# Small loads ahead of x, the first scale table shared between GpSimd and VectorE, later tables cut into pieces, and one more hidden tile prepared ahead, in a two-FFN-and-attention kernel on Trainium2

## What is computed

```
x = x + 0.5 * FFN(layernorm(x))
x = x + Attention(layernorm(x))        # one head of 128, softmax over 1024 keys, with biases
x = x + 0.5 * FFN(layernorm(x))        # the same FFN weights

FFN(x) = (silu(x @ Wg) * (x @ Wu)) @ Wd          # 512 -> 1376 -> 512
W[k, n] = scales[g_idx[k], n] * (w4[k, n] - (z4[g_idx[k], n] + 1))
```

## Time and profile before

| | us |
|---|---|
| median of 3 runs | 855.09 |
| lowest, highest | 853.18, 855.42 |
| the profiled execution, its own time | 856.05 |
| its span in the trace | 854.2 |
| TensorE busy | 831.7 (97%) |
| VectorE busy | 484.9 (57%) |
| ScalarE busy | 273.0 (32%) |
| GpSimd busy | 247.9 (29%) |

### The profile page before, as it was taken

The page is one execution under the profiler, slowest core; times in us unless marked ns, Lnnn a source line. Parts: engine busy times, 40 slices in busy tenths (PEclk is TensorE's granted clock), DMA queues, the critical chain, the costliest instruction groups (busy, mean ns, idle before and its releaser), DMA issues.

```text
span 854.2 us, 10686 instructions
## 1 busy us (share of the span) xinstructions
PE 831.7 (97%) x4006; PEld 675.2 (79%) x4006; DVE 484.9 (57%) x807; ACT 273.0 (32%) x469; POOL 247.9 (29%) x205
## 2 busy tenths in 40 slices
PE   4899999999999999999999999999999999999998
PEld 3676768887888888788888888888888888888786
DVE  5878664654845454464967686545445744434452
ACT  3222332453421121241574783111212512112221
POOL 6634431552210533030234463150510201101100
PEclk9999999999999999999999999999999999999999
DMA  5767656985484534142115146845344064444121
GB/s 149 213 228 225 220 167 216 356 316 191 179 315 143 162 135 144 57 161 86 62 62 168 67 162 251 314 136 172 125 149 162 25 221 137 159 148 150 39 95 54
DMA packets 71177, 139.28 MB, mean 163 GB/s; under 512 B 24485, under 2 KB 35413, under 8 KB 66133
## 3 DMA queue, kind: packets, MB, share of 16 engines
q1 hardware_dynamic: 65858, 131.22, 45.9%
q10 hardware_dynamic: 5138, 6.95, 2.5%
q0 software_dynamic: 128, 0.41, 0.2%
HBM read 100.52 MB, written 37.95 MB: 162 GB/s over the span
## 4 chain that ended last, share of the span: by engine, by line
PE 71%; DVE 2%; DMA 1%; ACT 1%; issue 0%; POOL 0%; SPq 0%; ACTq 0%; POOLq 0%; DVEq 0%
PE ps L774 37%; PE ps L781 31%; PE ps L792 2%; PE ps L1184 1%; DMA xn<-stream 1%; DVE xn L1706 1%; DMA stream<-xres 0%; DVE stats L1683 0%; DVE pT L1672 0%; ACT pr L1532 0%; POOL t L2172 0%; ACT oT L1299 0%; DVE oT L1672 0%; DVE t L1672 0%; DVE hT L1672 0%
## 5 line engine op out<-in xcount | busy, mean ns | idle before, releaser
L774 PE MATMUL ps<-blk,ring 128*128 128x512 f32 (+1 forms) x1386 | 321.1, 390 | 0.1
L774 PEld LDWEIGHTS ps<-blk,ring 128*128 128x128 f32 (+1 forms) x1386 | 256.6, 185 | 58.4 <-DVE blk L1672 0.5
L781 PE MATMUL ps<-wd,hT 128*128 128x512 f32 (+1 forms) x1056 | 250.8, 392 | 0.9 <-DVE hT L1672 0.8
L781 PEld LDWEIGHTS ps<-wd,hT 128*128 128x128 f32 (+1 forms) x1056 | 196.8, 188 | 43.5 <-DVE hT L1672 1.2
L2215 POOL TENSOR_TENSOR h<-h,u 128x512 f32<-128x512 f32 (+1 forms) x33 | 42.8, 1297 | 325.7 <-ACT h L1425 325.7
L781 PE MATMUL ps<-xT,wp 128*128 128x512 f32 x480 | 117.2, 399 | 0.2 <-DVE xT L1672 0.2
L781 PEld LDWEIGHTS ps<-xT,wp 128*128 128x128 f32 x480 | 89.3, 190 | 21.9 <-issue 2.2
L1675 DVE TENSOR_TENSOR u<-ps,p1s 128x512 f32<-128x512 f32 (+1 forms) x66 | 45.4, 688 | 97.3 <-PE ps L774 97.3
L1425 ACT ACTIVATE h<-h 128x512 f32<-128x512 f32 (+1 forms) x33 | 20.9, 632 | 176.8 <-DVE h L1675 176.8
L1675 DVE TENSOR_TENSOR u<-ps,u 128x512 f32<-128x512 f32 (+1 forms) x66 | 45.6, 691 | 26.2 <-PE ps L774 25.2
L1675 DVE TENSOR_TENSOR h<-ps,p1s 128x512 f32<-128x512 f32 (+1 forms) x33 | 22.8, 691 | 63.7 <-PE ps L774 63.7
(11 more groups left out here) (132 smaller groups left out, 892.0 us busy)
## 6 DMA issues: line engine op xcount, KB each, us to landing
ring<-wsaved SPq DMA_DIRECT2D x29, 1024.0 KB, 5.1
ring<-wsaved SPq DMA_DIRECT2D x33, 768.0 KB, 4.4
wsaved<-wp SPq DMA_DIRECT2D x10, 1024.0 KB, 4.7
stream<-xres SPq DMA_DIRECT2D x32, 256.0 KB, 2.3
xn<-stream SPq DMA_DIRECT2D x8, 1024.0 KB, 7.5
xres<-stream SPq DMA_DIRECT2D x32, 256.0 KB, 3.7
wfull<-wf ACTq DMA_DIRECT2D x20, 256.0 KB, 2.5
wsaved<-wp SPq DMA_DIRECT2D x10, 512.0 KB, 3.1
```

The costliest lines, as they stand in the source:

```text
L774: mm = pe.matmul(ps[0:w, bank, :], ring[:, slot, which, a, kt, 0:w], blk[:, which, b, kt, :], start=not onto and kt == 0 and n == 0, stop= ...
L781: mm = pe.matmul(bank_ap, lhs(a), rhs(b), start=first and n == 0, stop=last and n == 2)
```

## The change

1. **Constants** move from GpSimd to VectorE, in front of everything VectorE did; there are eight increments of `s_cst` now.
2. **Loads.** On ScalarE's queue, `grp` and the gate scales (after `s_cst` 2) go ahead of x. SyncE loads only the up scales there. Unit 3 moves behind `table_d(0)`.
3. **Piece 0 of the scale table**: GpSimd makes `left`, VectorE makes `table` in one instruction. GpSimd cuts the down scales before its first power, not after its second.
4. **VectorE's order at the start**: the one-hot ahead of the statistics; `table` of piece 0 and `unpack(0)` ahead of the second `ln_shift`; piece 1 right behind `dequantise(0)`, ahead of `rows_lo`.
5. **Pieces 2 and 3** are split: `left` at tiles 2 and 4, `table` at tiles 3 and 5, each at the head of the tile.
6. **GpSimd's one-hot work for down** goes one unit earlier: the first columns before `w_lo(1)`, clamp of the rest before `w_lo(2)`, compare before `w_lo(3)`.
7. **keep_warm** 8 instead of 6 at the start.
8. **Bottom of pair 0**: block 1's fourth hidden tile is split in `plain_bottom`; ScalarE does its part between the two copies of the last weight block. Slots and the wait for them change with it.

```diff
-            return e % 3 if e < NT + 2 else (0, 2, 1)[e % 3]
+            return e % 3 if e < NT + 2 else (1, 2, 0)[e % 3]
-            return e - 1 if e == NT + 2 else e - 2
+            return e - 1 if e in (NT + 2, NT + 3) else e - 2
-        FIRST_STEPS, CUT_STEPS, ZERO_STEPS, SCALE_STEPS = 4, 5, PACK + 1, 2
+        FIRST_STEPS, CUT_STEPS, ZERO_STEPS = 2, 5, PACK + 1
-            return 2 * ZERO_STEPS + SCALE_STEPS * piece
+            return 2 * ZERO_STEPS + 1 + 2 * piece
-        def first_table_gu(pool, step):
-            _, left, dst = scale_cols(0)
-            step(lambda: pool.tensor_scalar(dst, upper(left), keep[S_ROWS, 1:2], None, ALU.mult))
-            step(lambda: pool.tensor_tensor(out=dst, in0=dst, in1=left, op=ALU.subtract))
-        def scales_gu(eng, step, piece):
-            s, left, dst = scale_cols(piece)
+        def left_gu_of(eng, step, piece):
+            s, left, _ = scale_cols(piece)
             step(lambda: eng.scalar_tensor_tensor(out=left, in0=upper(s), scalar=keep[S_ROWS, 0:1], in1=s,
                                                   op0=ALU.mult, op1=ALU.subtract))
+        def table_gu(eng, step, piece):
+            _, left, dst = scale_cols(piece)
             step(lambda: eng.scalar_tensor_tensor(out=dst, in0=upper(left), scalar=keep[S_ROWS, 1:2], in1=left,
                                                   op0=ALU.mult, op1=ALU.subtract))
+        def load_scales(eng, m):
+            thrice = scales[m].rearrange("(o g) n -> o g n", o=1).to_broadcast([3, GK, INTER])
+            eng.dma_start(sc_gu[FOLD * m:FOLD * m + 3 * GK, :], thrice).then_inc(d_cut_gu, 16)
@@ sync
-            sp.dma_start(grp[:, :], groups).then_inc(d_grp, 16)
             sp.wait_ge(s_cst, 2)
-            for m in range(2):
...
+            load_scales(sp, 1)
...
-            load_units(sp, [1, 2, 3])
+            load_units(sp, [1, 2])
             sp.wait_ge(s_cut, FIRST_STEPS + CUT_STEPS)
             table_d(sp, 0)
-            load_units(sp, [4, 5])
+            load_units(sp, [3, 4, 5])
@@ tensor
-                    pe.wait_ge(s_cut, FIRST_STEPS)
-                if m == 0 and i:
+                if m == 0:
...
-            keep_warm(6)
+            keep_warm(8)
@@ scalar
                 copy(t_blocks(i)[:, 0:4:2, 0, :, :], fp32_t(t13, i)).then_inc(s_th13, 1)
+                if j == NT - 1:
+                    plain_hi(1, 3)
...
-                    if q or i > 2:
+                    if q or i > 3:
...
             act.dma_start(zq_d, flat(zeros[2], ZC_D)).then_inc(d_zq_d, 16)
+            act.dma_start(grp[:, :], groups).then_inc(d_grp, 16)
+            act.wait_ge(s_cst, 2)
+            load_scales(act, 0)
...
-            act.wait_ge(s_cst, 3)
+            act.wait_ge(s_cst, 4)
@@ vector
             def plain_top():
                 for i in range(NT):
+                    if i in (2, 4):
+                        left_gu_of(dve, tables, 1 + i // 2)
+                    if i in (3, 5):
+                        table_gu(dve, tables, 1 + i // 2)
...
-                    if i in (2, 4):
-                        scales_gu(dve, tables, 2 if i == 2 else 3)
...
-                    if i == 0:
-                        scales_gu(dve, tables, 1)
...
                 first_blocks_lo(NT - 1)
+                plain_lo(1, 3)
...
-                    if q or i > 2:
+                    if q or i > 3:
...
+            constants = maker(dve, s_cst)
+            constants(lambda: dve.memset(idx[Z_ROW:FOLD, GU_COLS], 0))
+            constants(lambda: dve.memset(sc_gu[S_ROWS, :], 0.0))
+            constants(lambda: dve.memset(mhalf[:, :], -0.5), lambda: dve.memset(keep[:, :], 1.0))
+            for row in (0, FOLD):
+                constants(lambda: dve.memset(keep[row:row + 2 * GK, 1:2], 0.0), lambda: dve.memset(keep[row:row + GK, 0:1], 0.0))
...
             clamp(dve, hots, GU_COLS, GK, H_ROWS)
+            dve.wait_ge(d_grp, 16)
+            compare_low(dve, hots, GU_COLS, 0, oh_gu[H_ROWS, :], H_ROWS)
+            one_hot(dve, hots, GU_COLS, 0, oh_gu[H_ROWS, :], H_ROWS)
             ln_stats(0, (0, 1))
             ln_var(0, (0, 1))
             ln_stats(0, (2, 3))
             ln_shift(0, (0, 1))
             ln_var(0, (2, 3))
-            dve.wait_ge(d_grp, 16)
-            compare_low(dve, hots, GU_COLS, 0, oh_gu[H_ROWS, :], H_ROWS)
-            one_hot(dve, hots, GU_COLS, 0, oh_gu[H_ROWS, :], H_ROWS)
-            ln_shift(0, (2, 3))
+            dve.wait_ge(s_cut, FIRST_STEPS)
+            table_gu(dve, tables, 0)
             dve.wait_ge(d_small, 32)
             unpack(0)
+            ln_shift(0, (2, 3))
             dequantise(0)
+            left_gu_of(dve, tables, 1)
+            table_gu(dve, tables, 1)
             rows_lo(0, (0, 1))
...
@@ gpsimd
-            constants = maker(pool, s_cst)
...
             pool.dma_start(sc_d, flat(scales[2], SC_D)).then_inc(d_cut_d, 16)
             cutter = maker(pool, s_cut)
+            pool.wait_ge(s_cst, 8)
             pool.wait_ge(d_cut_gu, 32)
             first_left_gu(pool, cutter)
+            pool.wait_ge(d_cut_d, 16)
+            cut_scales(pool, cutter, sc_d, rest_d, rest2_d, parts_d)
             deviation(0, 0, 2)
-            first_table_gu(pool, cutter)
             deviation(0, 2, RT)
...
             for u in range(UNITS):
-                if u == 2:
+                if u == 1:
...
+                if u == 2:
+                    clamp(pool, hots, DOWN_REST, GD)
                 if u == 3:
-                    clamp(pool, hots, DOWN_REST, GD)
-                if u == 4:
                     compare_low(pool, hots, DOWN_REST, 1, oh_d[:, P:D_COLS])
```

More of the change, by code:

```diff
@@ L618, in _ @@
                 sp.dma_start(idx[FOLD * m:FOLD * m + HOT_ROWS, GU_COLS], spread(g_idx[m], HOT_ROWS)).then_inc(d_idx_gu, 16)
-            sp.dma_start(grp[:, :], groups).then_inc(d_grp, 16)
             sp.wait_ge(s_cst, 2)
-            for m in range(2):
-                thrice = scales[m].rearrange("(o g) n -> o g n", o=1).to_broadcast([3, GK, INTER])
-                sp.dma_start(sc_gu[FOLD * m:FOLD * m + 3 * GK, :], thrice).then_inc(d_cut_gu, 16)
+            load_scales(sp, 1)
             sp.dma_start(idt[:, :], ident).then_inc(d_small, 16)
@@ L1995, in _ @@
             rows_lo(0, (2, 3))
-            dve.wait_ge(s_cst, 5)
             unpack(2)
@@ L2228, in bottom @@
                         sum_lo(q + 1, what, kt)
-            constants = maker(pool, s_cst)
-            constants(lambda: pool.memset(idx[Z_ROW:FOLD, GU_COLS], 0))
-            constants(lambda: pool.memset(sc_gu[S_ROWS, :], 0.0))
-            constants(lambda: pool.memset(mhalf[:, :], -0.5))
-            constants(lambda: pool.memset(keep[:, :], 1.0))
-            for row in (0, FOLD):
-                pool.memset(keep[row:row + 2 * GK, 1:2], 0.0)
-            pool.memset(keep[0:GK, 0:1], 0.0)
-            constants(lambda: pool.memset(keep[FOLD:FOLD + GK, 0:1], 0.0))
             pool.dma_start(sc_d, flat(scales[2], SC_D)).then_inc(d_cut_d, 16)
             cutter = maker(pool, s_cut)
+            pool.wait_ge(s_cst, 8)
             pool.wait_ge(d_cut_gu, 32)
             first_left_gu(pool, cutter)
+            pool.wait_ge(d_cut_d, 16)
+            cut_scales(pool, cutter, sc_d, rest_d, rest2_d, parts_d)
             deviation(0, 0, 2)
-            first_table_gu(pool, cutter)
             deviation(0, 2, RT)
@@ L2250, in _ @@
                 pool.dma_start(idx[row:row + FOLD, DOWN_COLS], spread(g_idx[2][first:first + D_COLS])).then_inc(d_idx_d, 16)
-            pool.wait_ge(d_cut_d, 16)
-            cut_scales(pool, cutter, sc_d, rest_d, rest2_d, parts_d)
             for u in range(UNITS):
-                if u == 2:
+                if u == 1:
                     pool.wait_ge(d_idx_d, 32)
```

## The result

The changed kernel takes **851.0 us** (median of 4 runs, 850.16 to 851.78) against 855.25 of the kernel before, run beside it (4 runs, 853.18 to 856.42): ratio 0.9953, interval 0.9931 to 0.9975. It is faster by 4.25 us, or 0.5%. The forecast was 849.3 with a range of 847.5 to 851.3: the time lies 1.7 above the forecast, near the upper end of its range, and the gain is 4.25 where 5.75 was added up. The profiled execution took 851.78 and has a span of 849.9, against 854.2: 4.3 us less.

A forecast was written before the change was run, and what follows sets the result against it. The prediction saw a latency-limited start, then a body following TensorE, busy 97%. Gains of 3.0 + 0.8 + 1.2 + 0.75 = 5.75 against the 855.09 us median gave 849.3, own range 847.5 to 851.3 (845.4 to 852.8 with rivals).

The forecast's parts named there:

- What bounds the kernel: Whole kernel: a latency-limited start, then a body following TensorE (97% busy); gains at the start and waits reach the end.
- The start: Up to the first product: it comes at 17.8 instead of 20.77, 3.0 us won, ends 1.7 and 4.0.
- I take 5.7, since what crowded them was x: At the start: scales put ahead of x land at 5.7, with x's fastest latency; 8.7 with the present one.
- with the same crowding 9.7; I take 9.7: At the start: x, issued 1.9 later, lands at 9.7; 9.2 if scales and x share the engines without harm.
- so the 1.0 us is covered: At the start: piece 1 ahead of `rows_lo` hides behind transposes ending near 16.8; uncovered it costs 1.0, up to 2.
- rival 2: Warming and VectorE's new work hold the start: 1.0 won there, tile 0 nothing, run 852.1; chance 0.17.
- rival 1: The whole wait at tile 1 goes, and the clock may not fall there: run 846.2; chance 0.22.
- End of tile 0: TensorE's wait of 2.20 at tile 1 shrinks to near 1.4: 0.8 us won, ends 0 and 1.3.
- The toss over the clash: End of tile 0: whether GpSimd's subtraction again runs beside `plain_lo`, costing 1.05; 0.53 was counted as won.
- Pieces 2 and 3: Tiles 2 to 5: split and put at heads of tiles, these steps are hidden; 1.2 us won, ends 0.6 and 1.2.
- Bottom: Bottom of pair 0: TensorE's wait for the fourth hidden tile's low part goes; 0.75 us won, ends 0 and 0.75.
- rival 3: Tile 0: GpSimd's clamp (2.41) and compare (2.3) each block VectorE once through the shared port, run 854.0; chance 0.06.

The follow-up runs named there:

- Experiment 3: Changed kernel with only the first 256 scale columns loaded ahead of x, the rest behind units 0 and 1: 849.32 us, ratio 0.9934.
- Experiment 7: Changed kernel with six warming products at the start in place of eight: 850.12 us, ratio 0.9939.
- Experiment 4: Changed kernel with GpSimd's compare of the remaining down columns moved back behind the fourth weight unit's subtraction: 849.40 us, ratio 0.9929.
- combined: Changed kernel with 256 scale columns ahead of x, compare behind the fourth subtraction, piece 1's table step behind the first `hs`: 847.43 us, ratio 0.9906.
- experiment 5: Changed kernel with pieces 2 and 3 made whole in tiles 2 and 4, as before: 851.46 us, ratio 0.9956.
- experiment 1: Changed kernel with both steps of piece 1 back behind the product of silu and up in tile 0: 850.47 us, ratio 0.9942.
- experiment 8: Changed kernel with the clears and constants back on GpSimd instead of VectorE: 850.14 us, ratio 0.9948.

## Why the prediction was right or wrong

**What bounds the kernel** was read rightly: what is won before and at a wait reached the end, and nothing of it was lost behind tile 1. The 4.30 by which the last products are ahead is the 4.3 of the spans. The body's idle time went with the waits, and none of the new places became a bound.

**The start, 3.0 predicted, 1.32 measured.** This is the step that failed, in three terms, and the result lies below the 1.7 that was its low end.
- *"I take 5.7, since what crowded them was x"*, of the scales. They landed at about 8.2, and GpSimd began at 8.37, near the bad end of that term (8.7). Nothing of x stood in front of them; their own size is what takes the time. Experiment 3 with 256 columns has them at 5.4, and `left` at 5.60.
- *"with the same crowding 9.7; I take 9.7"*, of x. It landed at 12.35: issued 0.57 later than assumed (3.87; `sc_gu` was clear at 2.93 and not at 2.4) and its last tile was 6.8 in flight in place of 5.0. The prediction asked whether x crowds the scales and never what the scales do to x. So the second power came at 13.63 and not 10.9. That is 2.7 us, nearly the whole delay of the second shift, which ended at 14.87 and not at 12.0.
- *"so the 1.0 us is covered"*, of piece 1 ahead of `rows_lo`. It took 1.97 instead of 1.0, and TensorE waited 1.33. The price without cover, up to 2 with a subtraction beside it, stood in the text; it was used for rival 2 alone. The cover was assumed at 2.8 (VectorE free at 14.0, transposes ended at 16.8); VectorE came to piece 1 at 16.57 and the transposes ended at 17.14, so 0.6 was left of it, and the subtraction ran from 17.04 on beside the table step.

One gain the prediction gave only to rival 1. Sixteen warming matmuls, ended at 13.61 with the lookups 0.47 behind, had the clock at 2.4 GHz for the transposes: together 1.4 us shorter than in the earlier trace rows's kernel (1.09 and 1.36 for 1.97 and 1.92). Experiment 7 shows that nothing of it came through, as the clash stood behind it. `shift` landed at 9.8, beyond the 6.8 to 9.5 assumed, which alone would put the lookups at 13.6; it and the table (13.93) ended almost together. This is rival 2's start ("1.0 won" by it, 1.32 measured) more than the forecast's, and the time of 851.0 is nearer to rival 2's 852.1 than to 849.3.

**End of tile 0, 0.8 predicted, 0.05 measured.** The wait shrank by 0.40 of the 0.8. The toss over the clash fell on the clash: `plain_lo` took 1.46, 0.77 more than its 0.69, and the clock went down behind the wait as the forecast left it in. On VectorE, from the start of `hs` to the end of `plain_lo`, 0.53 was won (3.37 before, 2.84 after): 0.25 of the 0.27 for piece 1's place, and 0.28 of the 0.53. The lead at tile 1 did not grow by it, since between the first product and the last products of tile 0 TensorE had given back 0.47 (the lead is 0.85 at 29.37, where before stands 30.22), 0.20 of it in a short wait that ended at 21.27 and that the kernel before does not have; the rest I have not traced. A sum that adds a gain at a wait must subtract what was lost on the way to it. Experiment 4 shows that the step's premise was right in kind: in another order of GpSimd's work the wait is 0.86, and with it the slow stretch goes (mean clock 0.999 or 1.0 in four runs), as rival 1 had it. That the shorter wait is the cause is not shown: `combined` waits 1.67 there, and its four runs have the same clocks.

**Pieces 2 and 3, 1.2 predicted:** 1.32 between the first down product and tile 4's, and 1.00 when undone in experiment 5. Right.

**Bottom, 0.75 predicted:** 1.09, and 1.03 when undone. Right in mechanism, short by 0.3, since a wait was costed at its gap alone. The trace of the kernel before shows where the rest lies. Products in a row start 0.23 apart and last 0.39, so each begins 0.16 before the last one ends; around the wait the starts are 1.14 apart, which is 0.91 lost and not 0.75. The first product behind the wait then lasts 0.50, and the next starts 0.11 late. TensorE shows no wait in the new slot either.

**Small rest:** 0.52 more is won behind pair 1's first product, which the prediction had at nothing. By the same products 0.30 of it comes in the attention stage, 0.14 at a single wait (0.29 at 411.41 before, 0.14 after), and 0.22 between 693 and 697 with no wait in it. That wait lies anywhere between 0.03 and 0.51 in the profiles of the experiments, so this is rather a difference between executions than the change.

**Luck.** The two failed steps fell short by 1.68 and 0.75. Pieces, bottom and this rest gave 0.98 more than predicted, and over half of that had no reason in the prediction. The time fell into the stated range with this help. That range was said to come from the ends of the start; these, 1.7 and 4.0, give 850.6 and 848.3, and 851.0 lies outside them.

**The shared port** (rival 3, 0.06) was rightly held improbable in its full form, and half true. The Trainium skill (SBUF — State Buffer, "Who interferes with whom") has a VectorE step with two SBUF inputs fully blocked by a GpSimd step that reads SBUF. The subtractions agree nearly in every kernel: 1.46 to 1.56 for steps of 0.47 that begin within about 0.1 us of one, and 1.46 for one of 0.69. The compare does not agree in size: blocked by it from 28.78 to 30.66 in experiment 4, `plain_lo` would have ended 0.69 behind that, at 31.35; it began at 29.05 and ended at 30.11, 0.37 over its 0.69.

The prediction held the clamp to be free, because piece 1's step ran in 0.48 near the end of it. The same trace has a line that it did not use. VectorE's one-hot began 0.12 behind the clamp's start (28.30) and took 0.80, where it takes 0.34 in experiment 4:

```profile
28.42 0.80 DVE L499 SCALAR_TENSOR_TENSOR oh_d<-idf,grp,oh_d 128x128 bf16<-128x128 f32 x1
```

So the clamp and the compare do cost something, but only to a step that begins soon after them.

## What to carry to other kernels

When a small load is put ahead of a large one, count its landings and the bytes that each carries, and cut it to the columns that the first user reads: here the cut was worth 1.3 to 1.8 us at the first product, about as much as the reordering itself. A step moved on VectorE is costed with the GpSimd step that will run beside it, by laying both timelines next to each other, and not by its clean duration; the two such places here account for 1.09 (experiment 1) and 0.94 us (experiment 4) of TensorE's waiting. Where several waits follow each other, remove the one that stands last in the chain first, or the gains of the others (here the warming) only make it longer.

## What the runs showed of the hardware that was not expected

- The slow stretch behind a wait comes in some executions and not in others. With the wait at tile 1 at 1.80 or 1.81 the granted clock fell in the profiled runs of the changed kernel, and it stayed at 1.00 in those of experiments 3 and 7; with 2.26 in experiment 1 it stayed too. With 0.86 (experiment 4) and with 1.67 (`combined`) the mean granted clock was 0.999 or 1.0 in all four runs. So the length of the wait alone does not decide. Over the 13 runs of the kernel before in the first group, those with a mean granted clock of 1.0 average 854.3 us (5 runs) and those with 0.998 average 855.9 (6 runs): 1.6 us, close to the 1.55 that the prediction read from the earlier trace rows for one such stretch. Over all three groups it is 1.4 (11 and 14 runs). The few runs of the changed kernel and of experiments 7 and 8 do not show it: their fastest runs, 850.16, 849.89 and 849.32, have 0.998, 0.998 and 0.997.
- A wait of TensorE costs about 0.3 more than its gap (0.75 gives 1.09, and 0.73 gives 1.03). Half of that is the overlap of 0.16 between products in a row, and 0.11 is the longer first product behind the wait.
- Two loads of 64.5 KB with three landings each, ahead of the four 256 KB tiles of x, made these slower in flight: median 5.7 in place of 4.0 or 4.1, and 5.2 to 5.9 in the other profiles with this start.
- GpSimd's compare beside a VectorE step with two SBUF inputs cost that step 0.37 to 0.54 (1.06, and 1.17 in `combined`, for 0.69; 0.88 for 0.34), where a subtraction costs it 0.8 to 1.1. In these cases of the compare, and at the clamp (0.80 for 0.34), the step ended as if it had begun 0.6 to 0.8 us behind the start of GpSimd's instruction. Piece 1's steps, begun 1.56 and 2.07 behind the start of the clamp, ran clean (0.47 and 0.48).
